# One transpose of q instead of two, its maxima by DMA, the output product in float16 halves, and a new order for the beginning and the last products

## The reference, cut to what matters

```
x = x + 0.5 * moe(layernorm(x))      # 8 experts, hidden 512, top-p weights
x = x + attention(layernorm(x))      # 16 heads of 16, 4 kv heads, causal
x = x + 0.5 * moe(layernorm(x))      # the same expert weights again

# moe: out += (silu(x @ gate_w[e].T) * (x @ up_w[e].T)) @ down_w[e].T * w[:, e]
# attention: q, k, v = x @ W.T + b; q and k RMS-normed and rotated; q * gain
#   out = softmax(q @ k.T / 4, causal) @ v ; return out @ Wo.T + bo
```

## Time and profile before

| | |
|---|---|
| median of 3 runs | 1164.36 us (1163.97 to 1164.65) |
| profiled execution | 1165.05 us, of which the span of the trace is 1162.9 us |
| PE busy | 1140.2 us, 98% |
| PE weight loads | 688.5 us, 59% |
| DVE busy | 804.0 us, 69% |
| POOL busy | 668.5 us, 57% |
| ACT busy | 575.3 us, 49% |
| mean granted TensorE clock | 0.997 |

### The profile page before, as it was taken

One profiled execution on the slowest core, in us unless ns is written; L12 is line 12 of the kernel. 1 busy time (PEld: TensorE's weight loads), 2 busy tenths in 40 slices (PEclk: granted clock), 3 DMA queues, 4 the chain that ended last, 5 costly groups with the idle time before them and its releaser, 6 DMA issues.

```text
span 1162.9 us, 23008 instructions
## 1 busy us (share of the span) xinstructions
PE 1140.2 (98%) x8161; PEld 688.5 (59%) x8161; DVE 804.0 (69%) x1993; ACT 575.3 (49%) x954; POOL 668.5 (57%) x737
## 2 busy tenths in 40 slices
PE   5899999999999999999999999999999999999998
PEld 2466555665565665665665666665656666656565
DVE  7878887678788677677677777767767455554443
ACT  4545544444555655555555555555455554333332
POOL 4545444368387677668667668658656464332322
PEclk9999999999999999999999999999999999999999
DMA  5411210000000000000000000000000000000000
GB/s 182 130 56 55 73 51 1 1 1 2 1 1 2 1 2 2 1 1 1 2 1 1 1 1 2 10 10 1 1 2 5 15 2 1 1 19 1 1 1 19
DMA packets 10109, 19.25 MB, mean 17 GB/s; under 512 B 2192, under 2 KB 6800, under 8 KB 10000
## 3 DMA queue, kind: packets, MB, share of 16 engines
q1 hardware_dynamic: 10000, 17.80, 4.7%
HBM read 15.70 MB, written 2.10 MB: 15 GB/s over the span
## 4 chain that ended last, share of the span: by engine, by line
PE 89%; DVE 0%; issue 0%; DVEq 0%
PE YB L330 27%; PE G L311 26%; PE U L311 26%; PE S L490 2%; PE S L467 2%; PE S L397 1%; PE S L505 1%; PE S L441 1%; PE S L407 1%; PE S L449 1%; PE S L378 0%; PE S L435 0%; PE S L499 0%; PE S L386 0%; PE S L417 0%; PE S L330 0%
## 5 line engine op out<-in xcount | busy, mean ns | idle before, releaser
L1103 POOL TENSOR_TENSOR HS<-TS,HS 128x512 f16<-128x512 f32 x256 | 300.4, 1173 | 396.6 <-ACT HS L564 395.6
L311 PE MATMUL G<-XS,W 128*128 128x512 f16 x1536 | 376.3, 381 | 0.9 <-ACT XS L594 0.9
L330 PE MATMUL YB<-W,HS 128*128 128x256 f16 x3036 | 373.8, 273 | 3.3 <-DVE X L748 2.6
L311 PE MATMUL U<-XS,W 128*128 128x512 f16 x1536 | 375.0, 380 | 0.8 <-DVE W L833 0.8
L727 DVE SCALAR_TENSOR_TENSOR TS<-TS,G 128x512 f32<-128x512 f32 x256 | 175.2, 684 | 241.9 <-ACT TS L557 241.7
L330 PEld LDWEIGHTS YB<-W,HS 128*128 128x128 f16 x3036 | 289.9, 98 | 75.1 <-DVE X L748 5.9
L564 ACT ACTIVATE HS<-TS 128x512 f16<-128x512 f32 x256 | 161.0, 629 | 250.9 <-DVE TS L732 250.5
L557 ACT ACTIVATE TS<-G,TSC 128x512 f32<-128x512 f32 x256 | 175.5, 686 | 209.9 <-PE G L311 202.7
L311 PEld LDWEIGHTS U<-XS,W 128*128 128x128 f16 x1536 | 150.7, 98 | 183.8 <-issue 2.7
L311 PEld LDWEIGHTS G<-XS,W 128*128 128x128 f16 x1536 | 146.6, 98 | 134.8 <-issue 2.9
L732 DVE SCALAR_TENSOR_TENSOR TS<-TS,U 128x512 f32<-128x512 f32 x256 | 176.0, 687 | 29.6 <-DVE TS L727 2.3
(11 more groups left out here) (178 smaller groups left out, 840.4 us busy)
## 6 DMA issues: line engine op xcount, KB each, us to landing
room<-in_gate SPq DMA_DIRECT2D x4, 512.0 KB, 3.2
room<-in_up SPq DMA_DIRECT2D x4, 512.0 KB, 3.3
room<-in_down SPq DMA_DIRECT2D x4, 512.0 KB, 3.9
QKT<-in_gate SPq DMA_DIRECT2D x4, 512.0 KB, 3.8
QKT<-in_up SPq DMA_DIRECT2D x4, 512.0 KB, 3.4
QKT<-in_down SPq DMA_DIRECT2D x4, 512.0 KB, 4.1
out_y<-X SPq DMA_DIRECT2D x16, 128.0 KB, 1.7
X<-in_x SPq DMA_DIRECT2D x3, 512.0 KB, 5.8
```

The source lines that it names most:

```text
L311: mm = eng.matmul(bank[:, :], W[:, e, wl, jj, kk * I + m * P:kk * I + (m + 1) * P], flat(XS16[:, b % 2, xl, kk, :, :], 'cq'), start=q == 0 ...
L330: mm = eng.matmul(out, HS[:, j % 2, hl, kk, m * P:(m + 1) * P], W[:, e, wl, 2, kk * D:(kk + 1) * D], start=kk + hl + wl == 0, stop=kk == K ...
L1103: eng.tensor_tensor(HS[:, j % 2, 1, m, :], TS[:, k % 3, :], HS[:, j % 2, 0, m, :], ALU.subtract).then_inc(L['g_lo'].sem, 1)
```

## The change

1. q is transposed once. ACT copies it straight to QKT, where `pe_max` reads it; QT1 and the zeroing `pool_qz` go. The maxima go as two halves of 16 heads into a small tile MM16, which one transpose turns to 32 rows; ACT copies these to MT16, and SyncE (SP) puts them by two DMAs (`sp_maxima`) into the rows of QKT that are theirs. `pe_scores` waits for the DMAs of its batch.
2. The output product: `dve_pv` writes float32 to a doubled RD, ACT makes its high half (`act_oh`), POOL its low half (`pool_ol`), 4 float16 transposes turn them, 6 float16 matmuls multiply with Wo, which is now scaled and split like the other weights. The column of ones in VS carries a scale. The copy and the product come one slot sooner behind the transposes (`O_STEP`).
3. The scales of weights come from one integer operation in place of a reciprocal and a product, and before the other small operations.
4. The beginning: new orders of the prologue on DVE, ACT, POOL and PE; other slots for tiles 4 to 7, for the router's first two products, for expert 0's down weights and for the preparations (`PREP`).
5. Some slots and steps of attention are moved by one or two.
6. The last four products: in banks S0, S1, S2, YB; two without their last quarter, these two's last quarters, then the other two whole.

```diff
--- before.py
+++ after.py
...
-PREP = [-99, 0, 8, 24, 36, 47, 58, 72, 83]
+PREP = [-99, 0, 14, 24, 32, 44, 60, 70, 83]
...
-AT = {'at': (108, 114, 16, 33), 'qkv': (110, 116, 21, 39), 'qt': (117, 124, 30, 48), 'kt': (118, 125, 32, 48), 'q2': (125, 137, 48, 69)}
-MAX0 = (119, 122, 126, 128, 130, 132)
-MAXB = (38, 41, 50, 56, 59, 66)
+AT = {'at': (108, 111, 16, 33), 'qkv': (110, 116, 21, 39), 'qt': (117, 124, 30, 48), 'kt': (118, 125, 32, 48), 'q2': (124, 137, 48, 69)}
+MAX0 = (119, 122, 126, 129, 131, 133)
+MAXB = (38, 41, 50, 57, 59, 66)
...
-FTP0 = (3, 3, 6, 6)
-FIRST_FTP = (99, 102, 104, 109, 152, 152, 161, 161)
-FTP_LATER, ROUTE_LATER = (22, 24)
-ROUTE_FIRST = (3, 11, 112, 162)
...
-A_STEP = {'ax': 3, 'xl': 3, 'bo': 6}
-Q_STEP = {'rb1': 2, 'sq': 2, 'rb0': 2, 'rr': 3, 'r': 4, 'qn': 5, 'qz': 4, 'v': 5, 'qh': 6, 'ql': 6}
-I_STEP = {'eb': 1, 'ea': 1, 'ma': 2, 'ec': 2, 'hb': 3, 'mc': 3, 'ha': 4, 'lb': 4, 'hc': 5, 'la': 4, 'lc': 5, 'pv': 7, 'o': 8}
+FTP0 = (3, 3, 5, 6)
+FIRST_FTP = (101, 102, 104, 107, 152, 152, 161, 161)
+FTP_LATER, ROUTE_LATER = (23, 24)
+ROUTE_FIRST = (0, 10, 112, 162)
+A_STEP = {'ax': 4, 'xl': 3, 'bo': 6}
+Q_STEP = {'rb1': 2, 'sq': 1, 'rb0': 2, 'rr': 3, 'r': 4, 'qn': 5, 'v': 5, 'qh': 6, 'ql': 6}
+I_STEP = {'eb': 1, 'ea': 2, 'ma': 1, 'ec': 2, 'hb': 3, 'mc': 2, 'ha': 4, 'lb': 4, 'hc': 5, 'la': 4, 'lc': 5, 'pv': 7, 'o': 8, 'oh': 9, 'ol': 9}
 R_STEP = {'r1': 1, 'ex': 1, 'r2': 1, 'r2b': 3, 'rank': 3, 'r3': 5}
-F_STEP = {'xn': 1, 'xh': 2, 'xl': 3}
-O_STEP = {'ot': 2, 'mm': 2, 'ad': 3}
+F_STEP = {'xn': 1, 'xh': 2, 'xl': 2}
+O_STEP = {'ot': 1, 'mm': 1, 'ad': 3}
...
-W_FIRST = {'mx': 1, 'wt': 2, 'wr': 4, 'wb': 5, 'sc': 5, 'hi': 6, 'lo': 6}
+X_FIRST = {'xn': (0, 0, 0, 0), 'xh': (1, 1, 1, 5), 'xl': (1, 1, 2, 4)}
+W_FIRST = {'mx': 0, 'wt': 1, 'wr': 3, 'wb': 5, 'sc': 5, 'hi': 6, 'lo': 5}
...
-OUTP = [FIRST + BATCH * (t // 2 + 1) + OUT[t % 2] for t in range(NT - 2)] + [ITEM[-1] + 9, ITEM[-1] + 13]
+OUTP = [FIRST + BATCH * (t // 2 + 1) + OUT[t % 2] for t in range(NT - 2)] + [ITEM[-1] + 11, ITEM[-1] + 15]
...
-        TAIL = (YB, S0, S1, S2)
+        TAIL = (S0, S1, S2, YB)
...
-            elif ks[0] == 0:
+            elif bank is YB:
...
         def pe_qtp2(eng, t, s):
             s0_read(eng, s)
             eng.wait_ge(*L['v_mm'].at(t, 'm2'))
-            for q in range(H // 2):
-                mm = eng.transpose(S0[:, :].bitcast(F16)[:, q * P:(q + 1) * P], flat(QS[:, t % 2, 2 * q:2 * q + 2, :, :], 'hsc'), ident16[:, :])
+            mm = eng.transpose(S0[0:2 * H, :].bitcast(F16)[:, 0:P], flat(MM16[:, :, :, :], 'shq'), ident16[:, :])
             mm.then_inc(L['p_q2'].sem, 1)
...
             s1_read(eng, s)
             s2_read(eng, s)
-            eng.wait_ge(*L['a_q2'].at(2 * b + 1, 'q'))
+            eng.wait_ge(s_mq, 32 * (2 * b + 2))
...
-            eng.wait_ge(*L['v_pv'].at(4 * (t // 2) + 3, 'ob'))
-            o = flat(OB[:, t // 2 % 2, t % 2, :, :], 'hc')
+            eng.wait_ge(*L['a_oh'].at(4 * (t // 2) + 3, 'oh'))
+            eng.wait_ge(*L['g_ol'].at(4 * (t // 2) + 3, 'ol'))
+            for q in range(2 * KD):
+                o = flat(O16[:, t // 2 % 2, t % 2, q // KD, :, :], 'hc')
+                mm = eng.transpose(S2[:, :].bitcast(F16)[:, q * P:(q + 1) * P], o[:, q % KD * P:(q % KD + 1) * P], ident16[:, :])
...
             for k in range(KD):
-                mm = eng.transpose(S2[:, k * P:(k + 1) * P], o[:, k * P:(k + 1) * P], ident[:, :])
-            mm.then_inc(L['p_op'].sem, 1)
-        def pe_op_mm(eng, t):
-            eng.wait_ge(*L['a_ot'].at(t, 'ot'))
-            for k in range(KD):
-                mm = eng.matmul(S2[:, D:2 * D], OT[:, k, :], WO[:, k, :], start=k == 0, stop=k == KD - 1)
+                for ol, wl in ((0, 0), (0, 1), (1, 0)):
+                    mm = eng.matmul(S2[:, D:2 * D], OT16[:, ol, k, :], WO16[:, wl, k, :], start=q == 0, stop=q == 3 * KD - 1)
+                    q += 1
             mm.then_inc(L['p_op'].sem, 1)
...
         def act_q2(eng, t):
-            qkt_freed(eng, t)
             eng.wait_ge(*L['p_q2'].at(t, 'q'))
-            eng.activation(flat(QKT[:, t // 2 % 2, t % 2, 0:H // 2, :], 'cq'), S0[:, :].bitcast(F16), ACT.Copy).then_inc(L['a_q2'].sem, 1)
+            if t:
+                eng.wait_ge(s_mq, 32 * t)
+            eng.activation(MT16[:, :], S0[0:2 * H, :].bitcast(F16)[:, 0:P], ACT.Copy).then_inc(L['a_q2'].sem, 1)
...
         def act_ot(eng, t):
             eng.wait_ge(*L['p_op'].at(t, 'tp'))
             eng.wait_ge(*L['p_op'].at(t - 1, 'mm'))
-            eng.activation(flat(OT[:, :, :], 'kq'), S2[:, 0:D], ACT.Copy).then_inc(L['a_ot'].sem, 1)
+            eng.activation(flat(OT16[:, :, :, :], 'hkq'), S2[:, :].bitcast(F16)[:, 0:2 * D], ACT.Copy).then_inc(L['a_ot'].sem, 1)
+        def act_oh(eng, i):
+            eng.wait_ge(*L['v_pv'].at(i, 'ob'))
+            eng.wait_ge(*L['p_op'].at(max(2 * (i // 4) - 3, -1), 'tp'))
+            eng.wait_ge(*L['p_w'].at(E, 'wb'))
+            eng.activation(O16[:, i // 4 % 2, :, 0, i % 4, :], flat(RD[:, i % 2, :, :], 'gc').rearrange('p (t c) -> p t c', t=2), ACT.Copy).then_inc(L['a_oh'].sem, 1)
...
-            eng.reciprocal(SCW[:, e % 2, :], PEW[:, :]).then_inc(lane.sem, 1)
+            eng.tensor_scalar(SCW[:, e % 2, :].bitcast(I32), PEW[:, :].bitcast(I32), -1.0, SC_BITS, ALU.mult, ALU.add).then_inc(lane.sem, 1)
             eng.tensor_scalar(TSC[:, e, :], PEW[:, 0:1], TANH_C, None, ALU.mult).then_inc(lane.sem, 1)
             eng.tensor_tensor(GUD[:, :], PEW[:, 0:1], PEW[:, 1:2], ALU.mult).then_inc(lane.sem, 1)
             eng.wait_ge(*lane.at(e, 'gu'))
             eng.tensor_scalar(CF[:, e:e + 1], GUD[:, :], PEW[:, 2:3], CF_C, ALU.mult, ALU.mult).then_inc(lane.sem, 1)
-            eng.wait_ge(*lane.at(e, 'rc'))
-            eng.tensor_scalar(SCW[:, e % 2, :], SCW[:, e % 2, :], 2.0 ** WTOP, None, ALU.mult).then_inc(lane.sem, 1)
...
-            eng.wait_ge(*L['p_qt'].at(t, 'q'))
+            mx = MXN[:, :, :, :].rearrange('p k g h -> p h (k g)')
+            eng.wait_ge(*L['p_q2'].at(t - 1, 'q'))
             eng.wait_ge(*L['v_mp'].at(MAXN[t], 'b'))
-            eng.tensor_copy(QS[:, t % 2, :, 3, 0], mx).then_inc(lane.sem, 1)
+            eng.tensor_copy(MM16[:, 0, :, :], mx).then_inc(lane.sem, 1)
             eng.wait_ge(*lane.at(t, 'm1'))
-            eng.tensor_tensor(QS[:, t % 2, :, 3, 1], mx, QS[:, t % 2, :, 3, 0], ALU.subtract).then_inc(lane.sem, 1)
+            eng.tensor_tensor(MM16[:, 1, :, :], mx, MM16[:, 0, :, :], ALU.subtract).then_inc(lane.sem, 1)
...
-            eng.tensor_reduce(RD[:, :, :], o[:, :, 0:3 * HD].rearrange('p g (s c) -> p g c s', s=3), AX.X, ALU.add).then_inc(lane.sem, 1)
+            eng.wait_ge(*L['g_ol'].at(i - 2, 'ol'))
+            rd = RD[:, i % 2, :, :]
+            eng.tensor_reduce(rd, o[:, :, 0:3 * HD].rearrange('p g (s c) -> p g c s', s=3), AX.X, ALU.add).then_inc(lane.sem, 1)
             eng.wait_ge(*lane.at(i, 'rd'))
-            eng.wait_ge(*L['p_op'].at(max(2 * (i // 4) - 3, -1), 'tp'))
-            eng.tensor_tensor(OB[:, i // 4 % 2, :, i % 4, :].rearrange('p t (g c) -> p t g c', c=HD), RD[:, :, :].rearrange('p (t g) c -> p t g c', t=2), RC[:, :].rearrange('p (t g) -> p t g', t=2).unsqueeze(3).broadcast_to([P, 2, G, HD]), ALU.mult).then_inc(lane.sem, 1)
+            eng.tensor_tensor(rd, rd, RC[:, :].unsqueeze(2).broadcast_to([P, 2 * G, HD]), ALU.mult).then_inc(lane.sem, 1)
...
+        def pool_ol(eng, i):
+            eng.wait_ge(*L['a_oh'].at(i, 'oh'))
+            eng.tensor_tensor(O16[:, i // 4 % 2, :, 1, i % 4, :], flat(RD[:, i % 2, :, :], 'gc').rearrange('p (t c) -> p t c', t=2), O16[:, i // 4 % 2, :, 0, i % 4, :], ALU.subtract).then_inc(L['g_ol'].sem, 1)
...
+        def sp_maxima(eng, t):
+            eng.wait_ge(*L['a_q2'].at(t, 'q'))
+            for half in range(2):
+                r = 3 * HD + half
+                eng.dma_start(QKT[r:r + 65:64, t // 2 % 2, t % 2, 0:H // 2, :], MT16[half * H:(half + 1) * H, :]).then_inc(s_mq, 16)
         def sp_slot(eng, s):
+            for t in due(QTP2, s, 1):
+                sp_maxima(eng, t)
...
-            for f in range(BT):
-                act_fx(eng, f)
+            act_fx(eng, 0)
+            act_fx(eng, 1)
+            act_fx(eng, 2)
             act_fc(eng, 0)
+            act_fx(eng, 3)
+            act_fc(eng, 1)
             act_w(eng, 0, 0)
-            for f in range(1, BT):
-                act_fc(eng, f)
+            act_fc(eng, 2)
             act_w(eng, 0, 1)
+            act_fc(eng, 3)
...
-            for f in range(BT):
-                dve_f_stats(eng, f)
-            for f in range(BT):
-                dve_f_aggr(eng, f)
-            eng.wait_ge(*L['v_fag'].at(BT - 1, 'aggr'))
-            eng.tensor_scalar(VEF[:, :], MVF[:, :, 1], LN_EPS, XS ** (-2), ALU.add, ALU.mult).then_inc(L['v_fep'].sem, BT)
+            dve_f_stats(eng, 0)
+            dve_f_stats(eng, 1)
+            dve_f_stats(eng, 2)
+            dve_f_aggr(eng, 0)
+            dve_f_aggr(eng, 1)
```

(55 more changed lines are left out.)

172 lines of the change are left out of this document (106 added, 66 removed), and 6 rows, old and new, of the table later.

## The result

The changed kernel takes 1151.53 us (median of 4 runs, 1150.95 to 1152.18), the kernel before, on the same chip, 1164.32: a ratio of 0.9889, 95% interval 0.9877 to 0.9902. That is 12.8 us faster, where 16.3 were forecast. The profiled execution took 1151.49 with a span of 1149.6, against 1162.9 before.

| stretch | before | after | gained | forecast |
|---|---|---|---|---|
| start to the fifth Y | 59.11 | 53.48 | 5.63 | 6.7 |
| from there to the end of the last regular Y (1153.59, 1141.56) | 1094.48 | 1088.08 | 6.40 | 8.6 (10.1 - 0.8 - 0.7) |
| tail | 9.31 | 8.04 | 1.27 | 1.0 |

What follows compares the result with a forecast made beforehand. PE, busy 98% of the span, was taken as the bound. Terms 10.1 + 1.0 + 6.7 - 0.8 - 0.7 gave 16.3 us saved, from 1164.36 to 1148.0 us; range 1144 to 1154.5.

Steps and rivals of the forecast that it cites:

- Second transposes: On PE in attention: eight second transposes of q become one, 0.39 us saved on each of 16 tiles, 6.2 us.
- Output product: Product with Wo on PE: six float16 matmuls replace float32, 0.215 us saved 16 times, 3.4 us.
- Its transposes: Before the product with Wo: four float16 transposes replace two float32 ones, 0 to 1 us saved, 0.5 taken.
- Tail: Last products of Y: new bank order removes a 0.74 us PE stop and shortens the chain behind; 1.0 us gained.
- Beginning: First G to fifth Y: new order removes stops and the half clock; 6.7 us gained, bounds 1 and 9.
- the walk: Queue-by-queue estimate of the new beginning: fifth Y at 51.4, 7.7 us sooner, with no DVE losses.
- the half clock: Beginning, third pair of G and U: PE at 1.2 instead of 2.4 GHz after stops, 2.8 us lost; expected to go.
- The rival that it comes at another pair: Beginning: PE's half clock stays or comes at another pair, another 2.8 us, 1150.8 us; chance 0.08.
- DMAs of the maxima: Before the first scores: PE stops once for 0.4 to 2.4 us, 0.8 lost; hidden in the seven later batches.
- the rival of late DMAs in every batch: DMAs land late in every batch, not hidden by 6.5 us; slower if stops reach 2.0 us each; chance 0.02.
- Tightened steps: Attention steps moved closer to their inputs: nothing to 0.3 us lost at each of 16 places, 0.7 taken.
- The rival of 5 us: Tightened steps stop PE in each batch, 5 us lost, 1152.3 us; chance 0.12.

Runs made afterwards that it cites:

- The run with 128 columns: Changed kernel with the maxima's tile 128 columns wide instead of 32, the rest zero, for its one transpose: 1148.63 us, ratio 0.9865.
- the run with two narrow ones: Changed kernel with its one 32-column transpose of the maxima issued twice in a row: 1152.44 us, ratio 0.9895.

## Why the prediction was right, and where it missed

The time lies in the forecast range and the sign is right. The median is 3.5 us above the forecast and outside the 1146 to 1150.5 that were given the most chance. Nearly all of the difference is in two terms, the transposes and the beginning; the misses on the output product, the tail and the DMAs went the other way and hid part of it, which was luck. Step by step:

- **Second transposes, forecast 6.2 us, got 3.1: the mis-sized term.** I priced one transpose as an eighth of a group of eight, 0.056 us, and reasoned from its moving columns alone. The 16 groups of eight took 7.2 us (0.45 each); the one takes 0.16, 2.6 in all, and makes the group before it 0.09 longer, 1.5 more. The run with 128 columns gives 2.9 of the missing 3.1 us back; the run with two narrow ones shows that the 0.10 belongs to each change of width.
- **Output product, forecast 3.4, got 3.9.** Its 16 steps went from 14.4 us in sum to 10.5. Seven of the steps before were 0.94 or 0.95, which the one row did not show; that they made up for part of the first term was luck.
- **Its transposes, forecast 0.5, got 0.2** (3.86 to 3.64 in sum): most of the float32 ones took 0.22 already.
- **Tail, forecast 1.0, got 1.27**; alone on the kernel before, 1.1 by the medians. Right in mechanism and size.
- **Beginning, forecast 6.7, got 5.63.** The walk's places came: first G 15.94 (15.6), second pair 21.36 (20.4), third 24.39 (23.5), L354 28.38 (28.0), fourth 29.36 (28.4), fifth Y 53.48 (51.4). The late half of the 2 us is at VectorE again: stops of 0.34 and 0.71 for its addition, which the walk had put at none and for which the sum took 1 us off. The walk also misread: of the three stops there only one, of 1.46 at 54.78, lies in the beginning; the others are at 127 and in the tail. The first maximum also came 0.45 later than in the profile before (first matmul at 8.16, there 7.71); in the other traces with this beginning it came at 7.73 to 8.09, so this is no part of the change. That the first pair stops for the copy of tile 3 costs nothing by itself: moved, the same time was lost at L370 and L354. That the half clock goes with the stop was right for the third pair only. The rival that it comes at another pair holds in four of the eight traces with this beginning, at 0.6 us to the fifth Y and not the 2.8 that it was given; that the trace of after shows none is luck.
- **DMAs of the maxima, forecast 0.8 lost, got nothing.** The landing was as taken. I counted the copy's start twice: the 0.72 from the earlier trace rows held the eight transposes themselves, and one transpose leaves 0.27. Without it the sum is 0.27 + 0.26 + 2.14 = 2.7 us, against the 2.86 from the transpose to the scores (304.61 to 307.47). Sent twice, the cover is gone and the stop is there, in the first batch alone: the rival of late DMAs in every batch had 6.5 us against it and they held. By the Trainium skill, page "DMA: Bandwidth & Descriptors", section "Anatomy of one DMA", the fixed cost of a DMA issued by GpSimd is about 2.0 us. These are SyncE's, and their 2.14 for two in a row, of 256-byte pieces, lies near that figure. Whether larger pieces would land sooner, no run shows.
- **Tightened steps, forecast 0.7 lost in 16 places, got 0.6 in one**: slot 117 (a stop of 1.64 us where before had 1.05), by `sq`, through the length of VectorE's operations beside POOL's and not through a late low half. The rival of 5 us did not come: with all the steps loosened no batch was faster behind that place. The 0.71 before the transposes of the normed tile, six times 0.1, has another cause, which stays open.

The stretch from the fifth Y on sums to 3.1 + 3.9 + 0.2 - 0.6 - 0.6, and 0.55 back for the stop for VectorE's addition at 127 us in the trace before, which stands again where the beginning was undone: 6.55 against the measured 6.40.

## What to carry to other kernels

A matmul is not priced by its columns alone: between groups look at when the load begins, and give a lone small transpose the stationary width of its neighbours, even with zeros, if it stands in a chain that PE bounds. When a copy shrinks, take its start anew from what now releases it. Where an engine is late only at places, shifting its work by slots can win without removing any (one number of `PREP` was worth 2.4 to 3.3 us here); check first what another engine then runs beside it. And read the beginning from several executions: one trace moved by a microsecond and missed the low clock that others had.
